# A graph layer on one core: norm roots moved to ScalarE, logits and late gates placed anew

## The reference

```
h      = layernorm(x)                          # 1250 x 512
scores = softmax(h @ Wgate)                    # 4 experts, the best 2 of each node are kept, weights w
q, k   = l2norm(silu(h @ Wq)), l2norm(silu(h @ Wk))    # 8 heads of 64; l2norm(x) = x * rsqrt(sum(x*x) + 1e-6)
v      = silu(h @ Wv);  beta = sigmoid(h @ Wb)
g      = -exp(A_log) * softplus(h @ Wa + dt_bias)
o      = scan over the nodes of each expert: S = exp(g) S + k (v - k S) beta; o = q S / 8
core   = sum over the node's experts of w * o
core   = core * rsqrt(mean(core*core over a head) + 1e-5) * o_norm_weight * silu(h @ Wg)
out    = x + core @ Wo
```

## Time and profile before

| | |
|---|---|
| three runs | 947.81, 947.84, 955.17 us; median 947.84 |
| the profiled execution | 953.01 us, span 951.2 us, mean granted clock 0.981 |
| busy, share of the span | PE 92%, DVE 65%, POOL 40%, ACT 27% |
| PE instructions (matmul) | 10668 |

### The profile page before, as it was taken

The page is one execution under the profiler, slowest core; times in us unless marked ns, Lnnn a source line. Parts: engine busy times, 40 slices in busy tenths (PEclk is TensorE's granted clock), DMA queues, the critical chain, the costliest instruction groups (busy, mean ns, idle before and its releaser), DMA issues.

```text
span 951.2 us, 24758 instructions
## 1 busy us (share of the span) xinstructions
PE 870.5 (92%) x10668; PEld 562.6 (59%) x10668; DVE 619.9 (65%) x1308; ACT 259.1 (27%) x462; POOL 383.1 (40%) x313
## 2 busy tenths in 40 slices
PE   3989999999999899999999968899999999898598
PEld 2544443445666444444444437888988999897343
DVE  7999999967887323233536445667766677664284
ACT  1221113201222000014113114444444444443331
POOL 6221100001111300000489837677666776662582
PEclk9999999999999899999999988999999999999889
DMA  8500000120000240000035754444444444422452
GB/s 243 162 0 1 1 1 1 44 66 1 1 1 1 79 165 0 1 0 1 3 84 240 281 201 114 120 109 133 133 114 133 121 136 125 116 64 47 122 152 67
DMA packets 74964, 80.54 MB, mean 85 GB/s; under 512 B 34452, under 2 KB 57670, under 8 KB 74853
## 3 DMA queue, kind: packets, MB, share of 16 engines
q1 hardware_dynamic: 69733, 57.78, 21.9%
q0 software_dynamic: 5120, 21.14, 6.3%
HBM read 54.44 MB, written 24.39 MB: 83 GB/s over the span
## 4 chain that ended last, share of the span: by engine, by line
PE 61%; DVE 20%; POOL 10%; issue 5%; DMA 2%; ACT 1%; SPq 1%; DVEq 0%; POOLq 0%
PE bank L834 10%; PE bank L765 9%; PE bank L859 5%; PE bank L568 4%; PE bank L1022 4%; PE bank L554 3%; POOL nrm L1320 3%; DVE rows L1490 3%; PE bank L756 3%; POOL qkv_slots L1325 3%; DVE rows L1619 2%; DVE rows L1492 2%; PE bank L850 2%; PE bank L935 2%; PE bank L922 2%
## 5 line engine op out<-in xcount | busy, mean ns | idle before, releaser
L756 PE MATMUL bank<-W,xT 128*128 128x512 f32 x296 | 128.3, 593 | 0.0
L756 PEld LDWEIGHTS bank<-W,xT 128*128 128x128 f32 x296 | 56.0, 190 | 69.9 <-issue 69.7
L765 PE MATMUL bank<-hs,big 125*125 125x512 f32 x200 | 86.6, 593 | 0.0
L1301 POOL TENSOR_TENSOR big<-big,ident_sb 125x125 f32<-125x125 f32 x10 | 11.4, 1140 | 173.8 <-ACT big L1085 173.8
L532 PE MATMUL bank<-W,xT 128*125 128x512 f32 x160 | 78.1, 602 | 0.0
L765 PEld LDWEIGHTS bank<-hs,big 125*125 125x125 f32 x200 | 37.3, 188 | 47.7 <-issue 47.4
L554 PEld LDWEIGHTS bank<-rows 128*126 128x126 f16 x360 | 43.5, 135 | 34.7 <-issue 24.2
L1625 DVE TENSOR_SCALAR rows<-iota_sb,tC 128x625 f16<-128x625 f16 x180 | 56.2, 379 | 10.5 <-PE bank L554 10.5
L834 PE MATMUL bank<-big 64*64 64x64 f32 x1600 | 58.4, 219 | 4.8 <-issue 3.7
L554 PE MATMUL bank<-rows 128*126 128x313 f16 x360 | 58.9, 299 | 4.2 <-DVE rows L1625 4.1
L1490 DVE TENSOR_SCALAR rows<-iota_sb,gbp 125x180 f16<-125x180 f16 x160 | 56.8, 355 | 0.0
(11 more groups left out here) (328 smaller groups left out, 1965.5 us busy)
## 6 DMA issues: line engine op xcount, KB each, us to landing
big<-qkv_slots SPq DMA_DIRECT2D x40, 256.0 KB, 3.5
rows<-step_rows SPq DMA_DIRECT2D x40, 128.0 KB, 3.2
rows<-gam_rows SPq DMA_DIRECT2D x40, 128.0 KB, 3.4
big<-qkv_slots SPq DMA_DIRECT2D x80, 64.0 KB, 2.8
big<-qkv_slots SPq DMA_DIRECT2D x40, 128.0 KB, 3.0
o_slots<-big SPq DMA_DIRECT2D x40, 128.0 KB, 2.9
x_all<-in_x SPq DMA_DIRECT2D x10, 224.0 KB
out<-tC SPq DMA_DIRECT2D x10, 224.0 KB
```

The costliest lines, as they stand in the source:

```text
L756: last = mm(bank[:, b0, :], xT[:, k, t * P:t * P + 128], W[:, w, k, :], start=(k == 0), stop=(k == KC - 1))
L765: last = mm(bank[0:P, t % 2, :], cnt[:, s, t * P:(t + 1) * P], hs[:, s, :], start=(s == 0), stop=(s == NT - 1))
```

## The change

Five edits, the first two with their helpers:

- The logits are made with the nodes as the stationary operand (`xT`, 125 columns) and the 20 columns of `wsm` as the moving one, so that they come out node by node in bank 5. The products stand singly or in pairs between the steps of the last two aggregations and of three feature products. `logit_rows`, `keep_logits`, `lgT` and the transposes go.
- The roots of the row norms go from POOL (power -1/2) to ACT (`Sqrt`), with a reciprocal on DVE behind. In the features ACT takes a tile's root behind the next tile's rows; in the output one tile at a time.
- `GAMMA_AT` is 4 instead of 2.
- `LATE` is 5 instead of 7: five output gates are made behind the scan. ACT's order in the output weaves them with the first tiles.
- The output goes by single tiles: PE transposes tile t + 1, then multiplies tile t.

```diff
-GAMMA_AT = 2
+GAMMA_AT = 4
-LATE = 7
+LATE = 5
...
+            def token_logits(t, k):
+                n = E + 2 * H
+                pe.wait_ge(S["xT_done"], NT + t + 1)
+                return mm(bank[0:P, 5, t * n:(t + 1) * n], xT[:, k, t * P:(t + 1) * P], wsm[:, k, :], start=(k == 0), stop=(k == KC - 1))
...
                     last = mm(bank[0:P, t % 2, :], cnt[:, s, t * P:(t + 1) * P], hs[:, s, :], start=(s == 0), stop=(s == NT - 1))
+                    if t >= 8 and 1 <= s < 9:
+                        token_logits(2 * (t - 8) + (s - 1) // KC, (s - 1) % KC)
...
+            project_rows(0, 2, (4, 5))
             for t in (8, 9):
                 transpose_row(1, t)
...
+            project_rows(1, 0, (6, 7))
+            project_rows(1, 1, (8, 9))
+            project_rows(1, 2)
             pe.wait_ge(W_loaded[3], 32)
+            pe.wait_ge(S["gate_exp"], 1)
             project_rows(0, 3)
...
-            for g in range(NT // 2):
-                for t in (2 * g, 2 * g + 1):
-                    gated_columns(t)
-                for t in (2 * g, 2 * g + 1):
-                    out_rows(t)
+            gated_columns(0)
+            for t in range(NT):
+                if t + 1 < NT:
+                    gated_columns(t + 1)
+                out_rows(t)
...
+            def row_norms(t):
+                act.wait_ge(S["ss_done"], t + 1)
+                A(nrm[:, t % 4, :], nrm[:, t % 4, :], ACT.Sqrt).then_inc(S["rn_done"], 1)
...
             feature_rows(0, 3)
+            row_norms(0)
             for t in range(2, NT):
                 for w in range(3):
                     feature_rows(t, w)
+                row_norms(t - 1)
                 if t == DECAY_AT:
                     decays()
             feature_rows(1, 3)
+            row_norms(NT - 1)
...
+            for t in range(LATE, LATE + 3):
+                late_gate(t)
+            for t in range(2):
+                weigh(t)
+            for t in range(2):
+                square(t)
+            late_gate(LATE + 3)
+            weigh(2)
+            late_gate(LATE + 4)
+            for t in range(NT):
+                root(t)
+                if t + 2 < NT:
+                    square(t + 2)
+                if t + 3 < NT:
+                    weigh(t + 3)
+                keep_columns(t)
...
-            def inverse_norm(t):
-                pool.wait_ge(S["ss_done"], t + 1)
-                G.tensor_tensor(nrm[:, t % 4, :], nrm[:, t % 4, :], phalf[:, 0:2 * H], ALU.pow).then_inc(S["rn_done"], 1)
...
                 dve.wait_ge(S["rn_done"], t + 1)
+                step(V.reciprocal(nrm[:, b, :], nrm[:, b, :]))
...
+            for t in range(LATE, LATE + 2):
+                gate_rows(t)
             for t in range(2):
                 mix_rows(t)
+            for t in range(NT):
+                moments(t)
+                if t + 2 < NT:
+                    mix_rows(t + 2)
+                finish(t)
+                if t in (1, 2, 3):
+                    gate_rows(LATE + 1 + t)
+                if t >= 2:
+                    last_sum(dve, V, t - 2)
```

More of the change, by code:

```diff
@@ L270, in gps_layer @@
         TF = [[unit(big, 8 + 11 * p + s) for s in range(2)] for p in range(2)]
[L271 removed]
+        lateT = [gbp[:, :, :].rearrange("p c n -> p (c n)"), iota[:, :].bitcast(f32)] + [xT[:, k, LATE * P:N] for k in (2, 3)]
         T0, TT, RES = (unit(big, 2 + n) for n in range(3))
@@ L735, in _, with project_rows @@
             pe.wait_ge(S["h_done"], NT)
[L737 to L747, removed]
+            def token_logits(t, k):
+                n = E + 2 * H
+                pe.wait_ge(S["xT_done"], NT + t + 1)
+                return mm(bank[0:P, 5, t * n:(t + 1) * n], xT[:, k, t * P:(t + 1) * P], wsm[:, k, :], start=(k == 0), stop=(k == KC - 1))
+            def project_rows(t, w, tiles=()):
                 b0 = feature_bank(t, w)
@@ L756, in project_rows @@
                     last = mm(bank[:, b0, :], xT[:, k, t * P:t * P + 128], W[:, w, k, :], start=(k == 0), stop=(k == KC - 1))
-                last.then_inc(S["f_psum"], 1)
+                    if k == KC - 1:
+                        last.then_inc(S["f_psum"], 1)
+                    if tiles:
+                        for i in range(2):
+                            small = token_logits(tiles[k // 2], k % 2 * 2 + i)
+                if NT - 1 in tiles:
+                    small.then_inc(S["logit_psum"], 1)
+            pe.wait_ge(S["small_loaded"], 64)
             for t in range(NT):
@@ L997, in _, with late_gate @@
             out_part(NCK - 1)
+            def late_gate(t):
+                if t == NT - 1:
+                    pe.wait_ge(S["f_act"], feature_count(LATE, 3))
+                for k in range(KC):
+                    last = mm(bank[0:P, (t - LATE) % 4, :], lateT[k][:, (t - LATE) * P:(t - LATE + 1) * P], W[:, 3, k, :], start=(k == 0), stop=(k == KC - 1))
+                last.then_inc(S["f_psum"], 1)
             for t in range(LATE, NT):
-                for k in range(KC):
-                    last = mm(bank[0:P, 1 + t - LATE, :], lateT[k][:, (t - LATE) * P:(t - LATE + 1) * P], W[:, 3, k, :], start=(k == 0), stop=(k == KC - 1))
-                last.then_inc(S["f_psum"], 1)
+                late_gate(t)
             pe.wait_ge(S["o_done"], NCK)
@@ L1228, in _, with late_gate @@
             keep_o(NCK - 1)
-            for t in range(LATE, NT):
+            def late_gate(t):
                 act.wait_ge(S["f_psum"], feature_count(t, 3))
-                A(hs[:, t, :].rearrange("p (b j e) -> p b j e", b=2, e=DH), by_halves(1 + t - LATE, P), ACT.Silu).then_inc(S["f_act"], 1)
+                A(hs[:, t, :].rearrange("p (b j e) -> p b j e", b=2, e=DH), by_halves((t - LATE) % 4, P), ACT.Silu).then_inc(S["f_act"], 1)
             def weigh(t):
@@ L1240, in square, with root @@
                 A(got(t, 1)[0:P, :], got(t, 0)[0:P, :], ACT.Square).then_inc(S["squared"], 1)
+            def root(t):
+                act.wait_ge(S["f_ms"], t + 1)
+                A(nrm[0:P, t % 4, 0:H], nrm[0:P, t % 4, 0:H], ACT.Sqrt).then_inc(S["rooted"], 1)
             def keep_columns(t):
@@ L1959, in finish @@
             def finish(t):
[L1960 removed]
+                dve.wait_ge(S["rooted"], t + 1)
+                step(V.reciprocal(nrm[0:P, t % 4, 0:H], nrm[0:P, t % 4, 0:H]))
                 V.tensor_tensor(tt3(got(t, 0)[0:P, :]), tt3(got(t, 0)[0:P, :]), bc(nrm[0:P, t % 4, 0:H], DH),
                                 ALU.mult).then_inc(S["f_gated"], 1)
+            for t in range(LATE, LATE + 2):
+                gate_rows(t)
             for t in range(2):
                 mix_rows(t)
[L1966 to L1979 removed]
+            for t in range(NT):
+                moments(t)
[6 more added lines that the diff above has]
+                    last_sum(dve, V, t - 2)
             for t in (NT - 2, NT - 1):
```

81 lines of the change are left out of this document (8 added, 73 removed).

## The result

| | changed kernel | kernel before | ratio, 95% interval |
|---|---|---|---|
| first comparison, 20 runs each | median 955.01 us (951.21 to 959.49) | 950.05 (944.48 to 961.41) | 1.0045 [1.0027, 1.0064] |
| profiled execution | 951.21, span 949.4, clock 0.980 | 953.01, span 951.2, clock 0.981 | |

The change makes the kernel slower by 0.45%, some 4 us. The forecast was 0.4 us faster, and 955.01 lies outside its range. 2.2 of the 7.6 us between 947.4 and 955.01 are the base: the median of before was 947.84 in the three runs shown and 950.05 in these twenty. What has to be explained is a step of +4.3 us by the ratio (5.0 by the medians; this text goes by the ratios) where -0.4 was forecast, and it is a puzzle: the two profiled executions say the opposite, 1.8 us faster.

The account below looks back on a forecast made before the run. POOL's chain, with PE almost as late, was taken to bound the features, and mostly PE the output. Features -1.8 and output +1.4 gave 952.6 us profiled, 947.4 at the median, range 942 to 953.

Parts of the forecast that it names:

- the features' -1.8: Features: the scan starts 2.3 us earlier, less 0.5 us for the first transposes at 1.2 GHz.
- Logits: Logits stage: small products at 0.10 each, 8.0 us in all; logits complete at 441.8 us, 3.0 later.
- B: Small products hide (0.05 each), last scatter lands at the median, PE's clock holds in the output: about 942.5 us; 17%.
- Gates, roots and tables: Gates and features: DVE's 4.41 us wait goes, `GAMMA_AT` costs nothing, roots with two 1.28 us loads take 2.8 a tile.
- D: A table switch costs ACT 2.7 us, not 1.3; tile 9's rows go 4 us later: +6.9, 954.5 us; 5%.
- E: Features: the gain is POOL's powers, ten of 2.93 us less 3.5 already hidden: some -25, 923 us; 1%.
- The wait for root 0: Features: PE idle 3.4 us near 461, tile 3 starts at 464.5, tile 9's last rows come 1.3 us later.
- rival C: Features: PE's clock falls at the new wait for root 0, costing 2.5 to 3.1 us; 950 up to 952 us; 19%.
- The clock ahead of the scan: Before the scan: PE idle 4 us against 1.2; 0.5 us given back for first transposes at 1.2 GHz.
- The five late gates: Output: two more late gates cost PE 6.9 us, mostly covered by its 10.44 us idle; output sum +1.4.
- Carrying one profile over to the median: Whole kernel: 952.6 us for the profiled execution, carried over to the median as 947.84 - 0.4 = 947.4 us.

Follow-up runs that it names:

- norms_alone: Kernel before with only the feature rows' roots moved to ACT and `GAMMA_AT` 4: 959.37 us, ratio 1.0043 to the kernel before.
- powers_late7: Changed kernel with the features' powers left on POOL, `GAMMA_AT` 2 and `LATE` 7: 947.88 us, ratio 0.9952 to the kernel before.
- late7_root0: Changed kernel with tile 0's root issued behind tile 2's feature rows and `LATE` 7: 949.27 us, ratio 0.9986 to the kernel before.
- root0_later: Changed kernel with tile 0's root issued behind tile 2's feature rows: 953.41 us, ratio 0.9993 to the kernel before.

## Why the prediction was wrong

The direction rested on a sum of -0.4 us, and in it on the features' -1.8: -5.3 us between the logits and the scan, of which -3.4 came. Each stage as the mean of three profiled executions of either kernel, in us:

| | before | change | difference | forecast |
|---|---|---|---|---|
| start to complete logits | 438.2 | 441.2 | +3.0 | +3.0 |
| logits to the scan's first products | 120.1 | 116.7 | -3.4 | -5.3 |
| scan, to the first late gate | 324.0 | 324.9 | +0.9 | +0.5 |
| late gates to the last sum | 64.3 | 65.1 | +0.8 | +1.4 |
| sum | | | +1.3 | -0.4 |

- **Logits** (right). 0.10 a small product was taken; the rows show four in 0.36 us net of overlap, 0.09, and pairs in 0.14, 0.07. B falls with this: it wanted 0.05, and a last scatter that lands by the median of 4.7 us, which took 6.72. The copy came at 441.56 for 441.8.
- **Gates, roots and tables** (right). The wait for the places went, `GAMMA_AT` cost nothing, a root took 0.22 us between two loads of 1.28, and no drain was seen: D falls. The Trainium skill (ScalarE: Activation LUTs, What ACT_TABLE_LOAD costs) gives 2.66 us for a switch with its drain; the load agrees with these rows, the drain doesn't. E fell too: the roots off POOL gave no gain of their own, 1.0043 and, without the wait, 0.9999.
- **The wait for root 0** (the step that failed). The text saw the 3.4 us of PE's idle time, priced them at 1.3 us, put the clock behind them at nothing in its sum and left it to rival C, at 19%. That rival is what happens in three executions of five, for 2.8, 3.0 and 1.4 us. Moving the root gives 2.4 us back in the change and 4.2 in the norm part alone. The length of a wait didn't tell here whether the clock falls: it also fell behind the wait of 1.64 us, where it happened to be free, and in `norms_alone` it didn't fall behind 2.43 us. C's time, 950 to 952, is 2.2 to 4.2 above the base of 947.84, and +4.3 was measured.
- **The clock ahead of the scan** (the mis-sized term). The gap was foreseen, 4 us, and was 5.3 to 5.6. It was given 0.5 us, for the first transposes. The low clock lasts longer than these: from the scan's first products to its fourth group of transposes 40.2 to 40.3 us in the three executions of the change, 39.5, 39.9 and 38.8 before. That is 0.85 us more than before, which had slow stretches there as well, and the scan as a whole was 0.9 longer: a small miss. But the term hid what the gap could have given: filled, it is worth 3.4 and 2.6 us by the ratios.
- **The five late gates** (right against before, wrong in what it compared). Covered by PE's 10.44 us, said the text. Against the kernel before the output comes out at +0.8 for +1.4. Against three late gates in the new order it costs 2.9 us in the output, and the gap ahead of the scan besides; only `powers_late7` shows this.
- **Carrying one profile over to the median.** This can't be mended by a better sum. The spans of one kernel's profiled executions lie up to 3.4 us apart (947.8 to 951.2 before, 949.4 to 952.4 for the change), and the first pair happened to be a late one of before and the fastest of twenty of the change. The clock of all executions agrees with the loss: a mean of 0.980 for before in each of five lists of 21 to 35, 0.978 for the change in each of three lists (42 in all), 0.982 to 0.984 with the gap filled. 0.002 of 950 us are 3.8 us more at half speed, at most 1.9 us of time, less than half of the 4.3.

**Open.** The stages give +1.3 of the +1.7 to +5.1 us that the three comparisons measured; with three profiles a side that is a mean uncertain by some 1.5 us (an estimate from the spans' spread of 3.4). So most of the +4.3 us isn't placed by a trace. The two waits fit the signs of all the repairs but `late7_root0`, and the repairs together, 8 to 12 us, are more than the two apart, 2.4 and 3.4.

The traces say where this difference may lie. With the later root, from the logits to the scan it took 112.0 to 112.3 us in the three executions with five late gates in which PE lost nothing to a stall of ACT, against 116.7 in the change. The scan took 318.4 to 323.1 us in the five executions with a filled gap, and 324.2 to 329.5 in the six with five late gates and an open one, 5.0 us between the means. `root0_later` has the early start and the open gap: its scan began 3.1 us before that of the change's first profile, then took 327.2 us, and the gain was gone. But of the 5.0 us only 2.0 lie ahead of the fourth group of transposes, where the gap's clock is; what shortened the rest of the scan isn't known. (One rival is untested: with the gap filled the scan starts directly behind the unused products, so what it reads may have had more time to arrive.) And whether ACT's stall costs the mean anything isn't known either.

## What to carry to other kernels

Where TensorE at its limit stands still at a stage's border, the cost is the wait and the slow stretch behind it, and the slow stretch may be hidden in one execution and not in the next; so compare means, or the clock of many executions, before believing a difference of 2 us between two profiles. Where the gap can't be closed, unused products in it were worth 0.3 to 0.7% here (0.3 and 0.4% with intervals that overlap, 0.6 and 0.7% on top of the later root, with intervals that part). In lists worked off in order, the first root or norm of a pipeline belongs behind the work that needn't wait for it, and a change made of five parts is worth taking apart: the logits and the single tiles with three late gates alone give 0.9952.

## What the runs showed of the chip

- Small products with their own stationary load (128x125, 20 columns) between large ones cost 0.09 us each in fours and 0.07 in pairs.
- A table load took 1.28 us, and where its input was ready the next activation started 0.01 to 0.02 us behind it (the loads at 462.29 and 538.85 in the change).
- The same wait of 1.64 us was followed by a clock of 0.50 in two executions of the change and by 1.00 in the third.
- With the 16 DMA engines full for 20 us, ScalarE stood for 5.2 to 11.3 us in 6 of 11 executions, some 5 to 8.5 of them with its input ready (an estimate from the rhythm of its rows, 3.43 us); smaller delays, 1.4 and 3.6 us, came with these engines nearly idle. The cause isn't shown.
